# Two attentions on one core: score matmuls in twos, their negated maxima turned two items later, the output copy one exponential earlier

## The reference

```
attn = softmax(einsum('bhqd,bhkd->bhqk', q, k) * scale)      # layer 1
scores = where(causal, scores, -inf); attn = softmax(scores) # layer 3
out = einsum('bhqk,bhkd->bhqd', attn, v)
```

## Time and profile before

| what | value |
|---|---|
| median of 3 runs | 471.08 us (470.23 to 471.4) |
| the profiled execution | 471.42 us, span of its trace 469.7 us |
| mean granted TensorE clock | 0.844 |
| busy: PE / DVE / ACT / POOL | 65% / 66% / 51% / 29% |
| layer 1 attention, steps | 196.4 us to 294.9 us |
| layer 3 attention, steps | 369.5 us to 445.5 us |

### The profile page before, as it was taken

How to read it: one execution, slowest core, us unless ns; L and a number is a source line. 1 busy time by engine, 2 the same in 40 slices (tenths; PEclk the granted TensorE clock), 3 DMA queues, 4 the chain that set the end, 5 groups by cost and what they waited for, 6 DMA issues and landing times.

```text
span 469.7 us, 5838 instructions
## 1 busy us (share of the span) xinstructions
PE 306.5 (65%) x1953; PEld 147.6 (31%) x1954; DVE 309.3 (66%) x791; ACT 241.0 (51%) x422; POOL 134.5 (29%) x237
## 2 busy tenths in 40 slices
PE   0014854532064636788888887876767899899686
PEld 0002722421023422112222232554443444344264
DVE  0678788777868666978888862343476778876230
ACT  3267844663375323256676678434243366765542
POOL 0112119751344530000000004118330244444420
PEclk9999975555556777579999999999797599999899
DMA  7950052000000043100000000000027000000001
GB/s 244 418 225 0 1 134 47 1 0 0 1 1 1 0 134 89 48 1 3 1 3 2 3 2 1 0 1 0 0 59 202 11 5 3 3 3 5 2 0 45
DMA packets 12139, 19.96 MB, mean 42 GB/s; under 512 B 2599, under 2 KB 11051, under 8 KB 11435
## 3 DMA queue, kind: packets, MB, share of 16 engines
q1 hardware_dynamic: 12108, 19.59, 13.2%
HBM read 12.51 MB, written 0.52 MB: 28 GB/s over the span
## 4 chain that ended last, share of the span: by engine, by line
PE 40%; DVE 32%; ACT 12%; POOL 7%; issue 7%; DMA 1%; SPq 1%; DVEq 0%; ACTq 0%; POOLq 0%
DVE nm L949 11%; PE ps L1471 9%; PE ps L1457 5%; PE pe L1383 4%; PE ps L1524 4%; PE pe L1493 4%; POOL rstd L343 2%; PE ps L1430 2%; DVE st L527 2%; ACT scr L1067 2%; DVE xn L537 2%; PE ps L1254 1%; DMA big<-in_wa 1%; ACT junk L1059 1%; PE pe L1348 1%
## 5 line engine op out<-in xcount | busy, mean ns | idle before, releaser
L949 DVE TENSOR_REDUCE nm<-ps 128x1 f32<-128x512 f32 (+2 forms) x224 | 131.8, 646 | 30.6 <-PE ps L1457 29.6
L1180 ACT ACTIVATE scr<-pe 128x1024 f32<-128x1024 f32 (+3 forms) x128 | 107.5, 867 | 75.7 <-PE pe L1493 74.6
L1457 PE MATMUL ps<-big 64*128 64x512 bf16 (+3 forms) x256 | 70.8, 377 | 11.7 <-DVE nm L949 11.7
L1471 PE MATMUL ps<-scr 128*32 128x512 f32 (+3 forms) x512 | 60.3, 543 | 9.0 <-ACT scr L1155 7.5
L343 POOL TENSOR_TENSOR rstd<-var,half 128x4 f32<-128x4 f32 x26 | 28.5, 1098 | 102.2 <-DVE var L532 77.4
L1493 PE MATMUL pe<-big 64*128 64x512 bf16 (+3 forms) x256 | 49.9, 360 | 2.2 <-ACT scr L1180 1.6
L443 POOL TENSOR_SCALAR_AFFINE_SELECT scr<-scr 128x256 f32<-128x256 f32 x64 | 25.7, 407 | 38.5 <-ACT scr L1180 37.2
L431 POOL CAST nm<-nm 128x16 bf16<-128x16 f32 x16 | 3.1, 196 | 116.2 <-DVE nm L949 116.2
L1457 PEld LDWEIGHTS ps<-big 64*128 64x128 bf16 x256 | 20.5, 99 | 39.0 <-DVE nm L949 33.7
L1493 PEld LDWEIGHTS pe<-big 64*128 64x128 bf16 x256 | 13.5, 94 | 53.1 <-ACT scr L1180 30.1
L537 DVE TENSOR_SCALAR xn<-x_tok,mv,rstd 128x128 f32<-128x128 f32 x60 | 17.1, 347 | 15.8 <-POOL rstd L343 15.8
(11 more groups left out here) (222 smaller groups left out, 582.8 us busy)
## 6 DMA issues: line engine op xcount, KB each, us to landing
big<-tern SPq DMA_DIRECT2D x48, 128.0 KB, 2.4
big<-in_wa SPq DMA_DIRECT2D x1, 2304.0 KB, 12.5
w<-in_w SPq DMA_DIRECT2D x2, 1152.0 KB, 19.3
big<-in_wa SPq DMA_DIRECT2D x1, 1344.0 KB, 6.2
big<-in_w SPq DMA_DIRECT2D x1, 1024.0 KB, 14.3
w<-in_w SPq DMA_DIRECT2D x1, 896.0 KB, 19.9
rowg<-in_rowg SPq DMA_DIRECT2D x1, 832.0 KB, 18.2
row<-in_row SPq DMA_DIRECT2D x1, 640.0 KB, 14.5
```

The costliest lines, as they stand in the source:

```text
L949: v.tensor_reduce(dst, src[:, 0:w * len(hs)].rearrange("p (h w) -> p h w", w=w), AX.X, ALU.max, negate=True).then_inc(sem(f"a{a}_max"), 1)
L1180: s_.activation(P[:, kt % 2, 2 * p:2 * p + 2, q0:S], E[(e - 1) % 2][:, :, q0:S], ACT.Exp, scale=SCALE).then_inc(sem(f"a{a}_p"), 1)
L1457: last = t_.matmul(dst[:, k * wd:(k + 1) * wd], stack_of(a, 0, b, HG * g + h, qt * 128, (qt + 1) * 128), stack_of(a, 1, b, HG * g + h, 0, ...
L1471: last = t_.matmul(bank[6][32 * h:32 * h + 32, q0:S], V[b][:, kt, HG * g + h, :], P[:, kt % 2, h, q0:S], start=(kt == 0), stop=(kt == TB - 1),
```

## The change

PE's loop over the 64 steps becomes a loop over 32 pairs: both score steps of a key tile are issued one after the other, then the items of the first step, then the value product of the key tile before, then the items of the second step. `LAG` goes from 2 to 4, so "parts" stands two items later in both PE's and DVE's lists. ACT's copy of bank 6 moves from ahead of a unit's fourth exponential to ahead of its third. Nothing is added or removed, and DMA issues keep their order.

```diff
-        LAG = 2
+        LAG = 4
@@
-                                if kt == 1 and p == 1 and u >= 1:
+                                if kt == 1 and p == 0 and u >= 1:
                                     unit_out(u - 1)
@@
-                    for s in range(64):
+                    def scores(s):
...
                         last.then_inc(sem(f"a{a}_sc"), 1)
-                        for x in slots[s + 1]:
+
+                    for k in range(32):
+                        scores(2 * k)
+                        scores(2 * k + 1)
+                        for x in slots[2 * k + 1]:
                             ring_item(*x)
-                        if p == 1 and s > 1:
-                            probs_out((s - 2) // 8, (s - 2) // 2 % 4)
+                        if k:
+                            probs_out((k - 1) // 4, (k - 1) % 4)
+                        for x in slots[2 * k + 2]:
+                            ring_item(*x)
```

## The result

The changed kernel takes 492.79 us (median of 4 runs, 492.35 to 496.63) against 471.12 us: 1.048 times as long, 95% interval 1.045 to 1.051, +21.7 us. 484.1 was forecast (+13.0), with a range of 477 to 497.

A forecast was written before the change was run, and what follows sets the result against it. A loop through PE, neither DVE nor ACT, was taken to bound both attentions. Layer 1 at -8.85 and layer 3 at +21.8 gave +13.0 on 471.08, so 484.1 us, range 477 to 497.

The forecast's parts named there:

- signs of being wrong: Layer 3 units under 10.5 us, or a granted clock under 1 in the middle of layer 3.
- Layer 1, the loop through PE cut, DVE the bound: Layer 1: two max items behind the value product keep DVE fed; unit 12.37 to 10.90 us, -8.85 us in all.
- Layer 1, LAG and the copy: Layer 1: later parts hides PE's 0.77 us wait, row DMA about fits; copy costs nothing; within the 10.9 us unit.
- Layer 3, first stretch: Layer 3, scores to first value product: no wait for the copy, 3.69 to 3.10 us a unit, -0.59.
- Layer 3, second stretch: Layer 3, first to second value product: waits for POOL's mark behind the parts, 3.26 to 4.05 us, +0.79.
- Layer 3, third stretch: Layer 3, second value product to next unit's scores: row DMA issued late, 2.28 to 5.26 us, +2.98.
- Unit of layer 3 at full clock: Layer 3: the three stretches add up to 12.41 us for 9.23, +3.18 a unit; layer 3 +21.8 us.
- The lower bound of +19: Layer 3's total loss if the row DMA takes 1.5 us from issue to landing: +19 us instead of +21.8.
- the first rival: TensorE's clock falls in layer 3, PE having two holes a unit: +10 us, 494 us; chance 0.20.
- Layer 1 without gain: Layer 1 gains nothing, the row coming late there too: 8.85 us more, 493 us; chance 0.07.
- a row in time in layer 3: Row of maxima lands in time in layer 3, unit only +0.2 us, so faster: 463.6 us; chance 0.09.
- no effect: The change does less since PE waits in other places anyway: within 0.3% of 471 us; chance 0.04.

The follow-up runs named there:

- order_alone: The kernel before with only PE's new pair loop, LAG 2 and the late copy kept: 493.16 us, ratio 1.046 to the kernel before.
- l3_marks_first: The changed kernel with POOL's marks ahead of the parts in layer 3: 469.34 us, ratio 0.996 to the kernel before.
- l3_lag2: The changed kernel with LAG 2 in layer 3 only: 470.36 us, ratio 0.997 to the kernel before.
- l3_filled: The changed kernel with matmuls adding zero put in front of PE's two waits in layer 3: 483.42 us, ratio 1.027 to the kernel before.
- l3_as_before: The changed kernel with layer 3's loop, LAG 2 and copy place of before, layer 1 as changed: 462.39 us, ratio 0.980 to the kernel before.
- lag_alone: The kernel before with LAG 4 and nothing else: 482.32 us, ratio 1.023 to the kernel before.

## Why the prediction was right

The direction, the two places and the full-clock sizes were right, but one term, TensorE's clock, was put at nothing in the sum and left to a rival. The total of 492.8 is 8.7 us above the forecast; it lies outside the band of 479 to 489 that had the chance of 0.60, and in the clock's band of 488 to 499 that had 0.20. It is inside the range because the range took in most of that rival. One of the prediction's own signs of being wrong came true: "a granted clock under 1 in the middle of layer 3".

- **Layer 1, the loop through PE cut, DVE the bound.** Right: unit 10.97 against 10.9, reductions in one piece. The sum was -8.85; by the ledger's rows it is -8.35 in the profiled execution, and the run with layer 3 untouched is 9.0 us faster by its median.
- **Layer 1, LAG and the copy.** Right, and more needed than the working said: by `order_alone`, the loop without them makes a unit of layer 1 longer than before. The prediction had costed the copy's new place at nothing in layer 1; alone it gains 0.23 us a unit, and with the pair loop it takes away a wait of 0.73 us.
- **Layer 3, first stretch.** Right: 3.02 against 3.10.
- **Layer 3, second stretch.** Right: 3.87 against 4.05, PE released by POOL's mark; `l3_marks_first` takes that wait away.
- **Layer 3, third stretch.** Right: 5.35 against 5.26, of which the DMA to the scores is 1.83 against 1.70 + 0.13; `l3_lag2` takes that wait away.
- **Unit of layer 3 at full clock.** 12.23 in `l3_filled` against 12.41, +20.0 us behind layer 1 against +21.8 for layer 3, and +12.0 in all against +13.0. The lower bound of +19 for a DMA of 1.5 us doesn't follow from the working: 0.2 us less in some six units is 1.2, which gives +20.6.
- **The clock.** Mis-sized: the forecast put it at nothing and left it to the first rival with a chance of 0.20, at +10. It did happen, in addition to the chains; by `l3_filled` it costs 9.4 us, close to the rival's price. The argument against it, that the units before had kept the clock, compared units with small holes to units with two long ones. The earlier trace rows had shown a fall behind windows none of which was wholly idle, and that should have weighed more.
- **The other rivals.** Layer 1 without gain is excluded by `l3_as_before`, a row in time in layer 3 by the wait of 1.21 us, and no effect by the total.

## What to carry to other kernels

An order that suits one loop may not suit its sibling: here one loop served two attentions that differ by a POOL step, and what made one 1.4 us a unit faster made the other 3 us a unit slower, before the clock is counted. Before an item is moved later, follow the whole chain to the next engine's list (a mark that stands behind other work of POOL, a copy behind reductions of DVE, a DMA of 1.8 us) and compare it with the work that PE still has before it needs the result. Where a change leaves TensorE two holes, here 1.8 and 1.2 us in every 12, count with its clock falling too, and give it a term in the sum.

## What the runs showed of the hardware that was not expected

Extra work made the kernel faster: 11 more matmuls of 512 columns a unit, in six of the eight units of layer 3, kept the grant at 1.00 through the middle of the layer and took off 9.4 us.

The number and length of the waits in a unit don't settle whether the clock falls. With 1.83 and 1.21 us of wait in 12.2 the grant fell three times between 384 and 450 us. With 1.19 us for the DMA in every 10.3 us (`l3_marks_first`), or 1.45 us at "parts" (`l3_lag2`), it stayed at 1.00 through the middle of layer 3. But it fell once there in `lag_alone`, with waits of only 0.89 us for the DMA and 0.61 us for ACT's copy in every 10.6, and in layer 1 of `order_alone`, with 0.73 and 1.49 us in 13.05. What tells these cases apart no run here shows.
